# Graph layer on one core: narrow one-hots on ScalarE, the edge count ahead of the gathered groups, the table in pieces

## What is computed

```python
xn = layernorm(x)
h = maxk(xn @ W_neigh, 32)                       # 32 largest of each row are kept
neigh = segment_sum(h[src], dst) / max(deg, 1)   # deg = edges per dst
x = x + (xn @ W_self + neigh) + mix(xn)          # mix: linear attention, gated, projected
sel = the 3124 rows with the largest layernorm(x) @ wr + br
x[sel] += ffn(layernorm(x)[sel]) * weight ; x += layernorm(x)
```

## Time and profile before

| what | value |
|---|---|
| runs | 2382.03, 2396.82, 2448.0 us (median 2396.82) |
| profiled execution | 2399.27 us, span in the trace 2397.4 us |
| outside the span | 1.87 us |
| busy in the span | TensorE 63%, VectorE 54%, GpSimd 46%, ScalarE 12% |
| mean granted clock of TensorE | 0.77 of full speed |

### The profile page before, as it was taken

How to read it: one execution, slowest core, us unless ns; L and a number is a source line. 1 busy time by engine, 2 the same in 40 slices (tenths; PEclk the granted TensorE clock), 3 DMA queues, 4 the chain that set the end, 5 groups by cost and what they waited for, 6 DMA issues and landing times.

```text
span 2397.4 us, 29660 instructions
## 1 busy us (share of the span) xinstructions
PE 1501.7 (63%) x6995; PEld 945.4 (39%) x6995; DVE 1299.9 (54%) x4748; ACT 288.2 (12%) x764; POOL 1113.5 (46%) x1260
## 2 busy tenths in 40 slices
PE   1995443555655566566554674765667677853998
PEld 0553431233333333343342342443444344532666
DVE  6999630554655266536635645645564765665111
ACT  1443200000000000001000101010011011100211
POOL 2455617566545346533535444536353553542312
PEclk8998765766777678776777776877777777875999
DMA  8221363233233223322223322323232232331201
GB/s 171 67 77 60 111 142 104 68 90 99 73 93 87 71 74 92 89 76 74 84 69 87 86 79 80 106 63 101 72 95 81 78 108 71 103 91 45 73 18 29
DMA packets 128351, 199.87 MB, mean 83 GB/s; under 512 B 37335, under 2 KB 89382, under 8 KB 128249
## 3 DMA queue, kind: packets, MB, share of 16 engines
q0 software_dynamic: 53616, 131.54, 19.3%
q10 hardware_dynamic: 38636, 40.69, 6.1%
q1 hardware_dynamic: 35997, 26.43, 5.1%
HBM read 162.33 MB, written 35.71 MB: 83 GB/s over the span
## 4 chain that ended last, share of the span: by engine, by line
another core or an unknown queue 28%; PE 28%; DVE 20%; issue 14%; ACTq 3%; DVEq 2%; ACT 2%; SPq 2%; DMA 0%; POOL 0%; POOLq 0%
PE bank L1099 6%; DVE region_k L1457 5%; DVE region_k L1456 4%; PE bank L1039 4%; PE bank L1146 4%; PE bank L1160 3%; PE bank L1052 3%; PE bank L953 1%; ACTq L461 1%; DVE region_r L1341 1%; PE bank L1025 1%; SPq L530 1%; DVE region_r L1337 1%; ACT region_k L869 1%
## 5 line engine op out<-in xcount | busy, mean ns | idle before, releaser
L722 POOL DMA_INDIRECT ring<-rows_d,stage x928 | 926.6, 998 | 944.7 <-PE bank L1052 577.8
L1039 PE MATMUL bank<-region_k 128*125 128x500 f16 x978 | 400.0, 505 | 524.1 <-ACT region_k L869 185.6
L1456 DVE TENSOR_SCALAR region_k<-iota,region_k 128x125 f16<-128x125 f16 x978 | 281.9, 288 | 517.1 <-remote 414.9
L1039 PEld LDWEIGHTS bank<-region_k 128*125 128x125 f16 x978 | 155.1, 166 | 751.8 <-issue 316.5
L1052 PE MATMUL bank<-ring,region_v 128*125 x1084 | 327.9, 427 | 59.4 <-issue 36.0
L1457 DVE TENSOR_SCALAR region_k<-iota,region_k 128x500 f16<-128x500 f16 x978 | 352.8, 361 | 12.6 <-issue 12.3
L1440 DVE SCALAR_TENSOR_TENSOR region_v<-iota,tile_start,dstT 128x500 f16 x271 | 198.3, 740 | 70.7 <-issue 43.7
L1052 PEld LDWEIGHTS bank<-ring,region_v 128*125 x1084 | 154.4, 142 | 150.3 <-issue 75.1
L869 ACT ACTIVATE region_k<-bank 125x500 f16<-125x500 f32 (+1 forms) x117 | 65.6, 577 | 1118.6 <-remote 868.4
L1053 PE MATMUL bank<-ones,region_v 128*125 128x2 f16 x1084 | 184.2, 170 | 20.8 <-issue 20.3
L1053 PEld LDWEIGHTS bank<-ones,region_v 128*125 x1084 | 156.8, 145 | 28.5 <-issue 28.5
(11 more groups left out here) (307 smaller groups left out, 1978.0 us busy)
## 6 DMA issues: line engine op xcount, KB each, us to landing
ring<-rows_d,stage POOLq DMA_INDIRECT x928
kept_d<-region_v ACTq DMA_DIRECT2D x50, 252.0 KB
region_v<-xT_d ACTq DMA_DIRECT2D x53, 125.0 KB
xT_d<-region_r ACTq DMA_DIRECT2D x51, 125.0 KB, 2.0
rows_d<-region_r SPq DMA_DIRECT2D x50, 125.0 KB
region_k<-in_x_dram ACTq DMA_DIRECT2D x50, 125.0 KB
out_dram<-region_v ACTq DMA_DIRECT2D x50, 125.0 KB
region_v<-in_x_dram SPq DMA_DIRECT2D x5, 1120.0 KB
```

The lines of the kernel that those rows point to most:

```text
L722: pool.indirect_dma_start(out=ring[:, c, :], out_offset=None, in_=rows_d, in_offset=bass.IndirectOffsetOnAxis(ap=stage[:, c:c + 1], axis=0 ...
L1039: m = pe.matmul(out, lo, key, start=(c == WINDOW_AT[unit.window]), stop=(c + 1 == WINDOW_AT[unit.window + 1]))
L1456: dve.tensor_scalar(lo, iota[:, 0:T], lo_staged[:, at, u:u + 1], None, ALU.is_equal)
```

## The change

**Narrow one-hots.** ScalarE makes them, one position early: for each chunk Abs(iota - lo) (L856 of the changed file), and for each piece of up to 8 chunks one Relu(1 - value) in place (L863; two where the ring of 32 wraps). ScalarE waits for its own Abs before the Relu (`s_far`) and releases the piece (`s_lo`). VectorE keeps the 978 wide one-hots, in 12 slots.

**Order.** On TensorE and on VectorE the count of a position comes ahead of its visits (or dense product), so ahead of the waits that open its sums. On ScalarE the units of position n+1 are staged and made at the end of position n, behind the evacuations of all windows closed so far, and the unit of window w waits for the evacuation of window w-2 first. The first position's are made ahead of the loop.

**Table.** SyncE no longer loads `table` in two transfers ahead of its loop; ScalarE issues it in ten pieces of two transfers, two pieces in each of the first five positions.

```diff
-            spread(sp, table, rows_t, s_table)
...
+            def low(unit):
+
+                act.wait_ge(s_staged, unit.number + 1)
+                for piece in PIECES_OF[unit.number]:
+                    if piece.at + piece.chunks > LO_HOT:
+                        free(act, piece.at + piece.chunks - 1 - LO_HOT)
+                    for c in range(piece.at, piece.at + piece.chunks):
+                        last = act.activation(lo_slots(c), iota[:, 0:T].rearrange("p (a t) -> p a t", a=1), ACT.Abs,
+                                              bias=lo_staged[:, unit.number % STAGED, c - unit.at:c - unit.at + 1])
+                    last.then_inc(s_far, 1)
+                    act.wait_ge(s_far, piece.number + 1)
+                    ends = min(piece.chunks, LO_HOT - piece.at % LO_HOT)
+                    for first, chunks in ((piece.at, ends), (piece.at + ends, piece.chunks - ends)):
+                        if chunks:
+                            last = act.activation(lo_slots(first, chunks), lo_slots(first, chunks), ACT.Relu, bias=ones[:, 0:1],
+                                                  scale=-1.0)
+                    last.then_inc(s_lo, 1)
...
+            for p in range(2):
+                act.wait_ge(s_rows[p], 16 * (NT // 2 + 1))
...
+            def load_table(n):
+
+                for b in range(n * TABLE_PER, min((n + 1) * TABLE_PER, TABLE_PARTS)):
+                    spread(act, table[:, b * XL // 2:(b + 1) * XL // 2, :], rows_t[:, b * XL // 2:(b + 1) * XL // 2, :], s_table)
...
+            def lows(at):
+                for unit in at.units:
+                    evacuate_to(unit.window - 2)
+                    stage(unit)
+                    low(unit)
...
-                for unit in at.units:
-                    stage(unit)
+                load_table(n)
                 act.wait_ge(s_m3, n + 2)
                 gate_open(n + 1)
-                for unit in at.units:
-                    if unit.last:
...
+                evacuate_to(last_closed(at))
                 gate_hidden(n + 2)
+                if n + 1 < NT:
+                    lows(at.after(1))
                 if n:
                     store_row(at.before())
...
@@ TensorE
                 for c in range(unit.at, unit.at + unit.chunks):
-                    lo, key = hot_slot(c)
+                    if c == unit.at or PIECE_OF[c] != PIECE_OF[c - 1]:
+                        pe.wait_ge(s_lo, PIECE_OF[c] + 1)
                     pe.wait_ge(s_hot, c + 1)
...
@@ VectorE
-                    dve.tensor_scalar(lo, iota[:, 0:T], lo_staged[:, at, u:u + 1], None, ALU.is_equal)
-                    dve.tensor_scalar(key, iota[:, 0:KEYS], key_staged[:, at, u:u + 1], None, ALU.is_equal).then_inc(s_hot, 1)
+                    dve.tensor_scalar(key_slot(c), iota[:, 0:KEYS], key_staged[:, at, u:u + 1], None, ALU.is_equal).then_inc(s_hot, 1)
```

More of the change, by code:

```diff
@@ L104, in build @@
     LW = T + 1
-    COUNT_HOT = 16
+    KEY_HOT = 12
+    LO_HOT = 32
+    PIECE = 8
     UNIT = 16
@@ L108, in build @@
     TURNS = 5
-    assert KEYS <= 512
+    TABLE_PARTS = 10
+    TABLE_PER = 2
+    assert KEYS <= 512 and TABLE_PARTS * XL // 2 == NT
     def window_chunks(w):
@@ L125, in build @@
             UNITS.append(Unit(len(UNITS), w, offset, held, WINDOW_AT[w] + offset, offset == 0, offset + held == chunks))
+    Piece = namedtuple("Piece", "number at chunks")
+    PIECES_OF = []
+    for unit in UNITS:
+        before = sum(len(pieces) for pieces in PIECES_OF)
+        PIECES_OF.append([Piece(before + p, unit.at + offset, min(PIECE, unit.chunks - offset))
+                          for p, offset in enumerate(range(0, unit.chunks, PIECE))])
+    PIECE_OF = {c: piece.number for pieces in PIECES_OF for piece in pieces for c in range(piece.at, piece.at + piece.chunks)}
     Spot = namedtuple("Spot", "dense tile units since")
@@ L147, in build @@
     POSITION = {spot.tile: n for n, spot in enumerate(ORDER)}
+    assert min(POSITION[t] for t in range(ND)) * TABLE_PER >= TABLE_PARTS
     DEG_MAX = 24 * CHUNK
@@ L425, in build @@
         s_table, s_staged, s_tables = sem("s_table"), sem("s_staged"), sem("s_tables")
+        s_far, s_lo = sem("s_far"), sem("s_lo")
         x_t = x_d.rearrange("(t p) c -> p t c", p=T)
@@ L512, in agg_bank, with lo_slots, key_slot, free @@
             return bank[(0, 4)[at.n % 2]][0:T, :]
-        def hot_slot(c):
-            return count_hot[:, c % COUNT_HOT, 0:T], count_hot[:, c % COUNT_HOT, LW:LW + KEYS]
+        def lo_slots(c, chunks=1):
+            return lo_hot[:, c % LO_HOT:c % LO_HOT + chunks, 0:T]
+        def key_slot(c):
+            return key_hot[:, c % KEY_HOT, :]
+        def free(engine, c):
+            closed = sum(c >= end - 1 for end in WINDOW_AT[1:])
+            if c + 1 in WINDOW_AT:
+                engine.wait_ge(s_counts, closed)
+            else:
+                engine.wait_ge(s_hot_free, c + 1 - closed)
         def h_psum(s):
@@ L1086, in position @@
                 mix_open(n + 1, (n + 1) % TURNS, n + 1, n + 2)
+                for unit in at_.units:
+                    count(unit)
                 if n:
@@ L1105, in position @@
                           skip_group_check=True).then_inc(s_agg, 1)
-                for unit in at_.units:
-                    count(unit)
             positions(position)
```

46 lines of the change are left out of this document (22 added, 24 removed).

## The result

The changed kernel takes 2502.02 us (median of 4 runs, 2494.01 to 2511.68), the kernel before 2398.78 beside it: a ratio of 1.0456, 95% interval 1.0386 to 1.0527. The profiled execution takes 2503.16 us with a span of 2501.2, 103.8 more than before. The forecast was 2365 and the range ended at 2470. All ratios here are taken from the runs within 1.5% of the fastest of their kernel, so they can differ a little from the quotient of two medians.

What follows compares the result with a forecast made beforehand. No engine was taken as the bound, but the gap between a run of gathers' end and the next visits. Terms -50 - 29 + 46 - 5 + 3 = -35 against 2399.3 gave 2365 us, range 2230 to 2470.

Steps and rivals of the forecast that it cites:

- Transitions across a dense position: Nine transitions: gate part and dense product go inside the run of gathers, only the count behind it; -50 us (-126 to +72).
- The jam: Semaphore updates aren't delivered while GpSimd issues gathers, from some 12 us after its run's start to its end.
- part 3: New order on TensorE and VectorE: -50 us across dense positions, -29 between gathered ones, +46 for gate parts caught in runs.
- The rest: Transitions between gathered positions: -29 us from counts behind the run, +46 for gate parts slipping into the jam; together +17.
- The start: Table loading: -5 us from earlier gather indices, +3 for the ten pieces in ScalarE's queue; together -2.
- ScalarE's price: Narrow one-hots on ScalarE: an Abs every 0.28 us, a Relu over 7x125 1.06, a window of 7 chunks 4.8 us.
- B: Rival: less traffic between VectorE and TensorE lets the count go on within runs of gathers; 2240 us (2180 to 2320), chance .28.
- C: Rival: ScalarE's chain decides in 44 third and later windows, 7.2 instead of 4.8 us each; 2470 us (2445 to 2520), chance .22.

Runs made afterwards that it cites:

- late_after_all: Changed kernel with VectorE's read of the degree held until the ring's gathers land, in all gathered positions up to 44: 2607.09 us in one run, on a late chip.
- experiment 5: Changed kernel, late chip: no count behind dense positions 2536.27 us, at most two units 2498.11; two units with lateness imposed 2571.63; and late_after_all.

## Why the prediction was wrong

**The step that failed** is "Transitions across a dense position": "+31.5, inside the run of gathers", "so the sums open at about +50", and their sum of -50. The term let a gate part of 5.9 us and a product of 13.8 us go on at full pace within a run. On a prompt chip TensorE does that (the product takes 13.8 us inside a run); on the late chip, for which the forecast was made, it doesn't. The nine gate parts and what TensorE waits around them took 145.1 us instead of 53, the nine products 206.6 instead of 124. So even where a product opened inside the run, at +16.4 to +20.8, it closed at +39 to +51, well behind the run's end. In position 19 the sums opened at +69.97. The nine transitions measured +79.6 for -50: 130 of the 139 us between the forecast's -35 and the +103.8 of the trace.

The prediction's own trace had this and I overlooked it. The jam was taken for late updates alone, which a product that waits for nothing need not fear. But in the kernel before, the product of position 28 opened inside a run as well:

```profile
1550.83 0.17 PE L1090 MATMUL bank<-zeros 128*125 128x2 f16 x1
...
1562.66 0.58 PE L1099 MATMUL bank<-region_r,region_k 125*125 125x512 f16 x1 [1.24 <-issue]
...
1580.90 0.20 PE L1103 MATMUL bank<-zeros 128*125 128x2 f16 x1
```

It took 30.1 us, and that of position 42 took 26.6. I had seen the same gaps in the gate part, priced them in one gathered transition of four, and not at all across the dense positions.

A second fault lies in the sentence of part 3 that the waits on VectorE's reading "come behind the count and are long met". Ahead of a dense product there is no count, and on a late chip the degree is often read only when the run is over. It held TensorE directly for 24.4 us, in four of the nine. With the late degree imposed on both kernels, on a prompt chip, the new order costs 65.5 us in the dense transitions, of which the 53 us estimated above are counts that only change the column, and nothing in total.

The count behind the product is what remains in the transitions either way: 124.5 us of them go away without it on a late chip, only to stand elsewhere. Its price was right, 14.5 us for 32 chunks and 13.8 measured (1226.58 to 1240.38); but I had let it begin at the end of the run, with the product already done. Why TensorE's instructions are slow in a run on one kind of chip, and whether that and the late updates are one thing, stays open.

**The rest**: +17 forecast, +28.7 measured; that the size was right is in part luck. The gate part lasted over 8 us, stretched in a run, in 21 gathered transitions where the forecast had 8. Imposing the degree's lateness alone gives -49.8, so something further of the late chip costs about 80 us there. The gate's matmuls with 1.0 to 1.8 us of idle time between them (L1084 at 1200.70, as in the earlier trace rows) belong to it, and short counts of the last third: from 40 to 41 it was 13.8 us before and 24.6 after. Neither was isolated; late_after_all was meant to and met a late chip.

**The start**: -2 forecast, -6.7 measured on the late chip, -17.1 on a prompt one.

**ScalarE's price**: 0.28 us an Abs forecast, 0.30 measured; a Relu of 875 elements 1.06 forecast, 1.03 measured; a window 4.8 for 4.58. Here the Trainium skill's rule (in "ScalarE: Activation LUTs", "Rules for kernel authors") that such arithmetic belongs on VectorE didn't decide: putting it back, with rings of 16 slots, cost 4% on prompt chips (1.030 on one against 0.990 on another) and 48 us with lateness imposed.

**The jam**, read from one trace, was right about the late updates on that chip, said too little of TensorE, and is no property of the kernel: on four other chips the same program runs in about 1885 us without it. I drew it as starting some 12 us into a run. The changed kernel's trace has updates of TensorE late already 5 us into it: the sums of position 16 close at 1133.69, the degree is read at 1160.78.

**Rivals.** B (fewer updates end the jam) didn't happen. C gave the right sign and range by a wrong mechanism: the window looked at took 4.58 us, not 7.2, and TensorE's count waited for the Relu in 24 places, 80.8 us in all, but for 3 us and more in only 8, not in all 44 as C had it. What I hadn't listed is that TensorE itself would crawl through the product inside the run.

On the prompt chips the change is worth -1.0% (0.9904), and the table alone -1.5%. No version tried beats the table alone there; on a late chip none of those tried (the changed kernel and the four of experiment 5) beats the kernel before, and the table alone wasn't among them.

## What to carry to other kernels

A term that hides work inside another engine's run needs a row that shows such work going on at full pace inside such a run; look for it in the trace before, where here it showed the opposite. When work is moved ahead of a wait, look at the places where that work is empty: there the wait is bare, and in this loop those nine places held the longest product. And when a trace has waits released by nobody on the core, measure the kernel on a second chip before a plan is built on them.

## What the runs showed of the hardware

The same program takes 1881 to 1888 us on four chips and 2399 to 2421 in two sessions elsewhere (medians; a factor of 1.27). Gathers come every 1.25 us on both kinds. Two things differ in a run of gathers. TensorE's semaphore updates are seen late: summed over the gathered positions, the degree is read 721 us behind the closing of the sums in the changed kernel on a late chip and 20 us on a prompt one. And TensorE's matmuls, though they wait for nothing, come up to 2.8 us apart: in position 13 on the late chip 15 of them ran in 14.7 us (982.8 to 997.5), in position 18 on a prompt chip 106 in 13.9 us (927.3 to 941.2), with the same 106 GB/s of transfers in both stretches. Outside a run the large product takes 13.8 us on the late chip too (1231.11 to 1244.91 before the change, granted clock 1.00), and 15.8 us in the changed kernel at 1207, where the granted clock was 0.87. What makes a chip late wasn't found.
